# Clipping attention scores after the exponential on VectorE, in place of two ScalarE passes before it

## Chip, core and metric

The kernel runs on one core of a Trainium2 chip. The metric is device time in microseconds (us) of one execution; lower is better. The engines are TensorE (PE in the profile; PEld is its weight load), VectorE (DVE), ScalarE (ACT), GpSimd (POOL) and SyncE (SP, which issues the DMAs).

## What is computed

The reference is one cross-attention layer followed by a quantised feed-forward layer, on x of shape 8 x 1024 x 512 with a context of 8 x 64 x 512:

```python
lat = layernorm(_layernorm(x)); ctx = layernorm(context)
q = lat @ Wq; k, v = split(ctx @ Wkv)            # 16 heads of 64
attn = einsum('bhnd,bhsd->bhns', q, k) * 64 ** -0.5
attn = clip(attn, -11.0, 11.0)
attn = softmax(attn, axis=-1)
x = x + einsum('bhns,bhsd->bhnd', attn, v) @ Wo + bo
xq = fake_quant(_layernorm(x))
h = fake_quant(silu(xq @ Wg) * (xq @ Wu))
x = x + h @ Wd
```

The change is about the clip of the scores to -11 .. 11, which stands before the softmax.

## The kernel before

**Three stages.** `weights` prepares the operands (its last VectorE instructions make the bias and scale of the scores and two constants, `keep.bounds`). `attention` does the first layer in 16 steps of 512 tokens. `ffn` does the second layer.

**A step of attention.** Wq and the keys of a batch are folded into one matrix M, and the values and Wo into another, VW. Step s computes on TensorE the 8 score tiles of group s (`score`, each 128 rows, which are 16 heads x 8 context positions, by 512 tokens; 12 matmuls a tile, because each operand is split in a high and a low fp16 part). Then it computes the four output tiles of the group before (`output(s - 1, t)`, 24 matmuls each). Between them, in fixed places of TensorE's queue, stand: fold products for a coming batch (`fold_keys` in odd steps, `fold_values` in even ones: one half behind output tile 0, the other behind tile 2), `denominators(s)` inside output tile 1, and `turn_back(s)` inside output tile 2. The PSUM buffers `ring` hold four score or fold tiles; a score tile t + 4 waits until ScalarE has read tile t.

**Order on each engine.** Every engine has one queue written out by hand, and semaphores are the only link.

- ScalarE, for each tile t of the step: `cap` (Relu from PSUM, with the scale and the bias, into the fp32 tile E), `high(s - 1, t + 2)` (the fp16 high part of a probability of the group before), `floor` (Relu in place), in odd t `high_y` (high part of a normalised row of the next group), `exp` (Exp in place). `cap` and `floor` together are the clip.
- VectorE, for each t, the "score stretch": `divide(s - 1, t + 2)` (E times the inverse denominator, which is in PSUM), `low(s - 1, t + 1)` (the fp16 low part), in even t `norm_rows(s + 1, t // 2)`, in odd t `low_y(s + 1, t // 2)`. Behind the 8 tiles: `unit_range` (a range of feed-forward weights), `take(s - 1, 0)`, four fold tiles, `invert(s)` (reciprocal and expansion of the denominators, for `turn_back`), `norm_stats` and `norm_aggregates` of group s + 2, `take(s - 1, 1)`, `norm_rstd`, `take(s - 1, 2)`, four fold tiles, `divide(s, 0)`, `take(s - 1, 3)`, `divide(s, 1)`, `low(s, 0)`.
- GpSimd: `add_up(s, t)` for t = 1 .. 7 adds the exponentials of the tiles for the denominators, as they come; from t = 4 on a `bias` (adds bo to x) stands behind each; at the end `round_unit` (rounds a unit of weights, in steps 0 to 14).

`denominators(s)` waits for the seventh addition. `turn_back(s)` waits for `invert(s)`.

Of the kernel before, what the change touches and what calls it, by code (L numbers as in the profile page):

```python
# [14 lines left out]
fp32 = mybir.dt.float32  # L15
# [3 lines left out]
ALU = mybir.AluOpType  # L19
ACT = mybir.ActivationFunctionType  # L20
AX = mybir.AxisListType

P = 128
# [71 lines left out]
def weights(nc, mem, sem, keep, vecs, ctx_in, ln_c_w, ln_c_b, wq, wkv, wo, kv_d):  # L95
# [5 lines left out]
    with mem as ctx:  # L101
# [119 lines left out]
        def _(dve):  # L221
# [107 lines left out]
            for c in range(DC):  # L329
# [10 lines left out]
            do(nc.vector.tensor_tensor(sel[:].rearrange("p (n s) -> p n s", s=KS), misc[:].rearrange("p (n s) -> p n s", s=KS),  # L340
                                       keep.own_row[:].rearrange("p (a s) -> p a s", a=1).broadcast_to((P, NCTX // KS, KS)),
                                       ALU.mult))
            do(nc.vector.tensor_reduce(keep.score_bias[:], sel[:].rearrange("p (n s) -> p n s", s=KS), AX.X, ALU.add))
            do(nc.vector.tensor_scalar(keep.score_bias[:], keep.score_bias[:], -1.0, CLIP, ALU.mult, ALU.add))
            do(nc.vector.memset(keep.bounds[:, 0:1], 2 * CLIP))
            do(nc.vector.memset(keep.bounds[:, 1:2], -CLIP))

            do(nc.vector.tensor_tensor(keep.score_scale[:], sc[:, WQ, 1:2], sc[:, K, 1:2], ALU.mult))
            do(nc.vector.tensor_scalar(keep.score_scale[:], keep.score_scale[:], -1.0 / (LN_GAIN * FOLD_GAIN), None, ALU.mult))
            do(nc.vector.tensor_tensor(keep.out_scale[:], sc[:, WO, 1:2], sc[:, V, 1:2], ALU.mult))  # L350
            do(nc.vector.tensor_scalar(keep.out_scale[:], keep.out_scale[:], 1.0 / (PROB_GAIN * FOLD_GAIN), None, ALU.mult))
            nc.vector.reciprocal(keep.out_unscale[:], keep.out_scale[:])
# [126 lines left out]
def attention(nc, ctx, sem, keep, x_in, w_gate, w_up, w_down, kv_d, fold_d, x1_d, gate_up_q, down_q):  # L479
# [32 lines left out]
    fold_spilled, fold_loaded = [sem(f"fold_spilled{k}") for k in range(4)], sem("fold_loaded")  # L512
    ln_step, ln_y, y_hi, y_lo = sem("ln_step"), sem("ln_y"), sem("y_hi"), sem("y_lo")
    y_turned = [sem("y_turned0"), sem("y_turned1")]
    scores, capped, floored, exps, sums = sem("scores"), sem("capped"), sem("floored"), sem("exps"), sem("sums")
    dens, rdens, rden_turned = sem("dens"), sem("rdens"), sem("rden_turned")
    prob, prob_hi, prob_lo = sem("prob"), sem("prob_hi"), sem("prob_lo")
    x_biased, x_scaled = sem("x_biased"), sem("x_scaled")
# [119 lines left out]
    def on_gpsimd(pool):  # L638
        nc.gpsimd.memset(magic[:, 0:1], MAGIC).then_inc(magic_set, 1)
        nc.gpsimd.memset(magic[:, 1:2], -MAGIC).then_inc(magic_set, 1)  # L640

        def round_unit(u):
            n = unit_size(u)
            pool.wait_ge(f_scaled, scaled_before(u + 1))
            wait(pool, f_spilled, 16 * u)
            nc.gpsimd.tensor_scalar(quant[:, 0:n], raw[:, 0:n], MAGIC, QMAX, ALU.subtract, ALU.min).then_inc(f_rounded, 1)

        def bias(g, t):
            pool.wait_ge(ln_y, 4 * g + t + 1)
            nc.gpsimd.tensor_tensor(x[:, g % 4, t], x[:, g % 4, t], keep.bo[:], ALU.add).then_inc(x_biased, 1)  # L650

        def add_up(g, t):
            pool.wait_ge(exps, 8 * g + t + 1)
            if t == 1:
                wait(pool, dens, g)
                nc.gpsimd.tensor_tensor(esum[:], E[:, g % 2, 0], E[:, g % 2, 1], ALU.add).then_inc(sums, 1)  # L656
            else:
                pool.wait_ge(sums, 7 * g + t - 1)
                nc.gpsimd.tensor_tensor(esum[:], esum[:], E[:, g % 2, t], ALU.add).then_inc(sums, 1)  # L659

        for t in range(TT):
            bias(0, t)

        for s in range(NG):
            more = s + 1 < NG
            for t in range(1, KT):
                add_up(s, t)
                if more and t >= 4:
                    bias(s + 1, t - 4)
            if s < UNITS:  # L670
                round_unit(s)

    def on_scalar(act):
# [19 lines left out]
            elif values_folded_in(s) is not None:  # L693
                fold_value(values_folded_in(s), u)

        def cap(g, t):

            act.wait_ge(scores, 8 * g + t + 1)
            if g % 2 == 1:
                act.wait_ge(fold_spilled[t // 2], 32 * ((g - 1) // 2) + 32)  # L700
            else:
                wait(act, prob_lo, 8 * (g - 2) + t + 1)
            k = 8 * (g // 2) + t
            nc.scalar.activation(E[:, g % 2, t], ring[t % 4][:], ACT.Relu, scale=keep.score_scale[:],  # L704
                                 bias=keep.score_bias[:, k:k + 1]).then_inc(capped, 1)

        def floor(g, t):

            act.wait_ge(capped, 8 * g + t + 1)
            nc.scalar.activation(E[:, g % 2, t], E[:, g % 2, t], ACT.Relu, scale=-1.0, bias=keep.bounds[:, 0:1]).then_inc(floored, 1)  # L710

        def exp(g, t):
            act.wait_ge(floored, 8 * g + t + 1)
            nc.scalar.activation(E[:, g % 2, t], E[:, g % 2, t], ACT.Exp, bias=keep.bounds[:, 1:2]).then_inc(exps, 1)  # L714

        def high(g, t):
            act.wait_ge(prob, 8 * g + t + 1)
# [23 lines left out]
        for s in range(NG):  # L741
            more = s + 1 < NG
            for t in range(KT):
                cap(s, t)
                if s > 0 and t < 6:
                    high(s - 1, t + 2)
                floor(s, t)
                if more and t % 2 == 1:
                    high_y(s + 1, t // 2)
                exp(s, t)  # L750
            for t in range(TT):
                for u in FOLD_AFTER[t]:
                    fold(s, u)
                if t == 0 and s < UNITS:
                    scale_unit(s)
                if more and t == 1:
                    rescale(s + 1)
                if t >= 2:
                    high(s, t - 2)
# [3 lines left out]
    def on_vector(dve):  # L763
# [39 lines left out]
        def fold(s, u):  # L803
            if keys_folded_in(s) is not None:
                fold_key(keys_folded_in(s), u)
            elif values_folded_in(s) is not None:
                fold_value(values_folded_in(s), u)

        def invert(g):
            dve.wait_ge(dens, g + 1)  # L810
            nc.vector.reciprocal(rtok[:].rearrange("p t h -> p (t h)"), pd[:, 0:TT * H]).then_inc(rdens, 1)
            dve.wait_ge(rdens, 2 * g + 1)
            nc.vector.tensor_copy(rexp[:], rtok[:].rearrange("p t (h a) -> p t h a", a=1).broadcast_to((P, TT, H, KS))).then_inc(rdens, 1)

        def divide(g, t):
            if t == 0:
                dve.wait_ge(rden_turned, g + 1)
            dve.wait_ge(exps, 8 * g + t + 1)
            nc.vector.tensor_tensor(E[:, g % 2, t], E[:, g % 2, t], pd[:], ALU.mult).then_inc(prob, 1)  # L819

        def low(g, t):
# [49 lines left out]
        for s in range(NG):  # L871
            more = s + 1 < NG
            ahead = s + 2 < NG
            for t in range(KT):
                if s > 0 and t < 6:
                    divide(s - 1, t + 2)
                if s > 0 and t < 7:
                    low(s - 1, t + 1)
                if more and t % 2 == 0:
                    norm_rows(s + 1, t // 2)  # L880
                if more and t % 2 == 1:
                    low_y(s + 1, t // 2)
            if s < UNITS:
                unit_range(s)
            if s > 0:
                take(s - 1, 0)
            if more:
                for u in FOLD_AFTER[0]:
                    fold(s, u)
            invert(s)  # L890
            if ahead:
                norm_stats(s + 2)
                norm_aggregates(s + 2)
            if more:
                if s > 0:
                    take(s - 1, 1)
                for u in FOLD_AFTER[1]:
                    fold(s, u)
                if ahead:
                    norm_rstd(s + 2)  # L900
                if s > 0:
                    take(s - 1, 2)
                for u in FOLD_AFTER[2]:
                    fold(s, u)
                divide(s, 0)
                if s > 0:
                    take(s - 1, 3)
                divide(s, 1)
                low(s, 0)
# [19 lines left out]
    def on_tensor(pe):  # L929
        def ring_free(s, t):  # L930

            if s == 0:
                pe.wait_ge(m_lo, 4 + t + 1)
            elif keys_folded_in(s - 1) is not None:
                pe.wait_ge(m_lo, 8 * keys_folded_in(s - 1) + 4 + t + 1)
            elif values_folded_in(s - 1) is not None:
                pe.wait_ge(v_lo, 8 * values_folded_in(s - 1) + 4 + t + 1)
            else:
                pe.wait_ge(capped, 8 * (s - 1) + 4 + t + 1)

        def score(g, t):
            if t == 0:
# [3 lines left out]
            if t < 4:  # L946
                ring_free(g, t)
            else:
                pe.wait_ge(capped, 8 * g + t - 4 + 1)
            for c in range(DC):  # L950
                ins = split_products(nc, ring[t % 4][:], M[:, 0, c, t], M[:, 1, c, t], yT[:, g % 2, 0, c], yT[:, g % 2, 1, c],
                                     c == 0, c == DC - 1)
# [15 lines left out]
        def fold_keys(b, c):  # L968
# [4 lines left out]
            if c >= 2:  # L973
                pe.wait_ge(m_lo, 8 * b + u - 2)
            elif b > 0:
                pe.wait_ge(capped, 8 * (2 * b - 1) + 4 + u + 2)
            w = slice(c * P, (c + 1) * P)
            for q in range(IC):
                for n, (i, j) in enumerate(SPLITS):
# [9 lines left out]
        def fold_values(b, k):  # L989
# [4 lines left out]
            if k >= 2:  # L994
                pe.wait_ge(v_lo, 8 * b + u - 2)
            else:
                pe.wait_ge(capped, 8 * (2 * b) + 4 + u + 2)
            for n, (i, j) in enumerate(SPLITS):
                for h in range(2):
                    at = slice(64 * h, 64 * h + 64)  # L1000
# [388 lines left out]
def program(nc, x, ctx_in, ln_l_w, ln_l_b, ln_c_w, ln_c_b, wq, wkv, wo, bo, clip_x, clip_down, w_gate, w_up, w_down, out):  # L1389
    with ExitStack() as ctx:  # L1390
# [11 lines left out]
        keep.row_scale = sb("row_scale", [P, 2, FT], fp32)  # L1402
        keep.score_bias = sb("score_bias", [P, NCTX // KS], fp32)
        keep.score_scale = sb("score_scale", [P, 1], fp32)
        keep.bounds = sb("score_bounds", [P, 2], fp32)
        keep.out_scale = sb("out_scale", [P, 1], fp32)
        keep.out_unscale = sb("out_unscale", [P, 1], fp32)
        keep.rows = sb("x1_rows", [P, NG * TT, 4], fp32)
# [82 lines left out]
```

## Time and profile before

| | us |
|---|---|
| median of 3 runs | 1416.24 (1415.93 to 1416.41) |
| profiled execution, its own time | 1416.41 |
| its span | 1414.4 |
| PE busy | 1292.3 (91%) |
| DVE busy | 1196.6 (85%) |
| ACT busy | 788.2 (56%) |
| POOL busy | 411.0 (29%) |

How to read it: times in rows are microseconds unless marked ns. Positions are counted from the start of the span. In the timeline a row has the start, the duration, the engine, the line of the kernel, the operation, what is written from what, and, in square brackets, how long the engine sat idle before it and which instruction ended that. Consecutive instructions of one engine overlap a little (some 0.09 us on DVE), so an engine's pitch is shorter than its durations. TensorE's matmuls are shown with 0.38 us and follow each other every 0.216 us. Attention's 16 steps begin at 147.3, the last ends about 895; the first score matmul of steps 1 to 15 stands at 186.19, 233.78, 279.51, 326.05, 371.78, 418.33, 464.06, 510.60, 556.33, 603.15, 648.88, 696.56, 743.38, 791.50 and 838.32.

### The profile page before, as it was taken

How to read it: one execution, taken by the hardware profiler on the slowest of the kernel's cores; microseconds unless marked ns; L12 is line 12 of the kernel's file. 1: busy time of each engine (PE TensorE's matmuls, PEld its weight loads, DVE VectorE, ACT ScalarE, POOL GpSimd, SP SyncE). 2: the span in 40 equal slices, each digit the busy share in tenths (PEclk: the TensorE clock that was granted, in tenths of full speed). 3: DMA queues.
4: the chain of work that ended last, by engine and by line, in shares of the span. 5: the costliest groups of instructions: out<-in, count | busy, mean ns of one | idle time of the engine just before them, and what ended most of it. 6: DMA issues, size and time to landing. Idle time of an engine off the chain costs nothing.

```text
span 1414.4 us, 20500 instructions
## 1 busy us (share of the span) xinstructions
PE 1292.3 (91%) x7692; PEld 608.0 (43%) x7692; DVE 1196.6 (85%) x2053; ACT 788.2 (56%) x1179; POOL 411.0 (29%) x285
## 2 busy tenths in 40 slices
PE   4881889999999999999999999599999999889997
PEld 4430335444444444544444444244444444334433
DVE  7766589988998898888898875688999999789996
ACT  1662775577557755676567554143434333498662
POOL 3001443453245423552355232000000000035555
PEclk9995889999999999999999999899999999989999
DMA  5115352363534724546337250757666642289995
GB/s 230 60 60 180 89 178 68 112 187 107 193 89 112 216 84 138 138 125 209 92 96 217 76 153 22 201 152 258 222 212 229 244 164 86 94 319 425 425 393 209
DMA packets 178434, 242.77 MB, mean 172 GB/s; under 512 B 121368, under 2 KB 140576, under 8 KB 167328
## 3 DMA queue, kind: packets, MB, share of 16 engines
q1 hardware_dynamic: 178336, 241.47, 51.8%
q8 instruction: 60, 0.98, 0.3%
q14 instruction: 38, 0.31, 0.1%
HBM read 121.90 MB, written 90.57 MB: 150 GB/s over the span
## 4 chain that ended last, share of the span: by engine, by line
PE 37%; DVE 32%; ACT 10%; issue 5%; DMA 4%; SPq 2%; POOL 0%; POOLq 0%; ACTq 0%; DVEq 0%
PE pg L1349 10%; PE pu L1355 10%; PE pu L1383 7%; DMA yT<-y 3%; DVE y L791 3%; ACT E L710 3%; ACT E L704 3%; DVE x L830 3%; DVE st L833 3%; DVE E L800 2%; DVE st L768 2%; DVE M L795 2%; DVE E L819 2%; ACT y L677 2%; DVE w L1321 2%
## 5 line engine op out<-in xcount | busy, mean ns | idle before, releaser
L1224 ACT ACTIVATE sg<-pg,gate_scale 128x512 f32<-128x512 f32 x176 | 121.0, 687 | 187.0 <-PE pg L1349 187.0
L73 PE MATMUL ring<-yT,M 128*128 128x512 f16 x512 | 195.8, 383 | 7.0 <-DVE M L795 4.6
L74 PE MATMUL ring<-yT,M 128*128 128x512 f16 x512 | 195.8, 382 | 0.0
L75 PE MATMUL ring<-yT,M 128*128 128x512 f16 x512 | 195.7, 382 | 0.0
L1349 PE MATMUL pg<-xqT,w 128*128 128x512 bf16 x704 | 181.6, 380 | 2.8 <-DMA xqT<-xq 2.1
L73 PE MATMUL po<-VW,p 128*128 128x512 f16 x480 | 182.2, 380 | 0.0
L75 PE MATMUL po<-VW,p 128*128 128x512 f16 x480 | 181.9, 379 | 0.0
L74 PE MATMUL po<-VW,p 128*128 128x512 f16 x480 | 181.9, 379 | 0.0
L1355 PE MATMUL pu<-xqT,w 128*128 128x512 bf16 x704 | 181.5, 380 | 0.0
L1383 PE MATMUL pu<-w 128*128 128x512 bf16 x704 | 158.2, 385 | 18.8 <-DVE w L1323 10.1
L659 POOL TENSOR_TENSOR esum<-esum,E 128x512 f32<-128x512 f32 x96 | 130.3, 1357 | 77.6 <-ACT E L714 77.5
L1283 DVE TENSOR_TENSOR hb<-pu,sg 128x512 f32<-128x512 f32 x176 | 120.8, 686 | 31.0 <-PE pu L1355 29.5
L823 DVE TENSOR_TENSOR p<-E,p 128x512 f16<-128x512 f32 x120 | 140.6, 1171 | 6.6 <-ACT p L722 6.5
L1241 ACT ACTIVATE hb<-hb,magic,hscale 128x512 f32<-128x512 f32 x176 | 125.2, 802 | 32.1 <-DMA hb<-hidden 28.2
L722 ACT ACTIVATE p<-E 128x512 f16<-128x512 f32 x120 | 74.9, 625 | 97.7 <-DVE E L819 95.5
L791 DVE TENSOR_TENSOR y<-y 128x512 f16<-128x512 f32 x64 | 55.6, 869 | 74.3 <-ACT y L677 74.3
L1287 DVE TENSOR_REDUCE hmax_g<-hb 128x1 f32<-128x512 f32 x176 | 117.7, 676 | 0.0
L656 POOL TENSOR_TENSOR esum<-E 128x512 f32<-128x512 f32 x16 | 20.4, 1274 | 331.9 <-ACT E L714 331.9
L1383 PEld LDWEIGHTS pu<-w 128*128 128x128 bf16 x704 | 68.4, 99 | 108.3 <-DVE sg L1328 14.6
L1349 PEld LDWEIGHTS pg<-xqT,w 128*128 128x128 bf16 x704 | 68.8, 98 | 87.1 <-DMA xqT<-xq 3.2
L1209 POOL PARTITION_ALL_REDUCE one<-one x2 | 0.7, 352 | 362.8 <-DVE one L1308 316.9
L1355 PEld LDWEIGHTS pu<-xqT,w 128*128 128x128 bf16 x704 | 69.1, 98 | 83.7 <-issue 1.1
(200 smaller groups left out, 2260.9 us busy)
## 6 DMA issues: line engine op xcount, KB each, us to landing
hidden<-hb SPq DMA_DIRECT2D x11, 2816.0 KB, 9.8
hb<-hidden SPq DMA_DIRECT2D x11, 2816.0 KB, 19.4
xa<-x_rows_d SPq DMA_DIRECT2D x28, 1024.0 KB, 6.3
x<-in_x_dram SPq DMA_DIRECT2D x16, 1024.0 KB, 5.8
value_fold<-E SPq DMA_DIRECT2D x64, 256.0 KB, 2.5
VW<-value_fold SPq DMA_DIRECT2D x16, 1024.0 KB, 6.2
x_rows_d<-x SPq DMA_DIRECT2D x16, 1024.0 KB, 5.0
out_dram<-xa SPq DMA_DIRECT2D x12, 1024.0 KB, 13.7
```

Source lines behind the costliest of these rows:

```text
L73: nc.tensor.matmul(out, a_hi, b_hi, start=first, stop=False)
L74: nc.tensor.matmul(out, a_hi, b_lo, start=False, stop=False)
L75: return nc.tensor.matmul(out, a_lo, b_hi, start=False, stop=last)
L659: nc.gpsimd.tensor_tensor(esum[:], esum[:], E[:, g % 2, t], ALU.add).then_inc(sums, 1)
L823: nc.vector.tensor_tensor(probs(g, 1, t), E[:, g % 2, t], probs(g, 0, t), ALU.subtract).then_inc(prob_lo, 1)
L1224: nc.scalar.activation(sg[:, n % 4], pg[n % 4][:], ACT.Silu, scale=gate_scale[:, n % FT:n % FT + 1]).then_inc(silus, 1)
L1241: nc.scalar.activation(hb[:, slot, m], hb[:, slot, m], ACT.Identity, scale=hscale[:, m:m + 1], bias=magic[:, 0:1]).then_inc(h_scaled, 1)
L1283: nc.vector.tensor_tensor(hb[:, HOME[g], i], pu[n % 4][:], sg[:, n % 4], ALU.mult).then_inc(hs, 1)
L1287: nc.vector.tensor_reduce(hmax_g[:, i:i + 1], hb[:, HOME[g], i], AX.X, ALU.max, apply_absolute_value=True).then_inc(reaches, 1)
L1349: ins = nc.tensor.matmul(pg[n % 4][:], wg[:, c, at], xqT[:, g % 2, c], start=(c == 0), stop=(c == DC - 1))
L1355: ins = nc.tensor.matmul(pu[n % 4][:], wu[:, c, at], xqT[:, g % 2, c], start=(c == 0), stop=(c == DC - 1))
L1383: ins = nc.tensor.matmul(pu[t][:], hq[:, q % 2, m, t * P:(t + 1) * P], wd[:, m], start=(m == 0), stop=(m == FT - 1))
```

## The change

ScalarE's `cap` and `floor` go. `exp` reads the scores from PSUM directly (with the scale and bias that `cap` had, sign changed), and a new VectorE instruction `clip` limits the exponentials in place to exp(-11) .. exp(11): one in-place fp32 instruction of 128 x 512 with two constants for each of the 128 tiles. GpSimd's additions wait for `clip` in place of `exp`; TensorE's reuse of a PSUM buffer waits for `exp` in place of `cap`. In VectorE's queue `clip(s, t)` stands behind `norm_rows` and ahead of `low_y`. `invert(s)` is moved behind `norm_stats(s + 2)` and `norm_aggregates(s + 2)` (steps 0 to 13 have these). In `weights` three small VectorE instructions for the bias and the constants go.

```diff
-            do(nc.vector.tensor_reduce(keep.score_bias[:], ...))
-            do(nc.vector.tensor_scalar(keep.score_bias[:], keep.score_bias[:], -1.0, CLIP, ALU.mult, ALU.add))
-            do(nc.vector.memset(keep.bounds[:, 0:1], 2 * CLIP))
-            do(nc.vector.memset(keep.bounds[:, 1:2], -CLIP))
+            nc.vector.tensor_reduce(keep.score_bias[:], ...)
...
         def add_up(g, t):
-            pool.wait_ge(exps, 8 * g + t + 1)
+            pool.wait_ge(clips, 8 * g + t + 1)
...
-        def cap(g, t):
+        def exp(g, t):
             act.wait_ge(scores, 8 * g + t + 1)
...
-            nc.scalar.activation(E[:, g % 2, t], ring[t % 4][:], ACT.Relu, scale=keep.score_scale[:],
-                                 bias=keep.score_bias[:, k:k + 1]).then_inc(capped, 1)
-        def floor(g, t):
-            act.wait_ge(capped, 8 * g + t + 1)
-            nc.scalar.activation(E[:, g % 2, t], E[:, g % 2, t], ACT.Relu, scale=-1.0, bias=keep.bounds[:, 0:1]).then_inc(floored, 1)
-        def exp(g, t):
-            act.wait_ge(floored, 8 * g + t + 1)
-            nc.scalar.activation(E[:, g % 2, t], E[:, g % 2, t], ACT.Exp, bias=keep.bounds[:, 1:2]).then_inc(exps, 1)
+            nc.scalar.activation(E[:, g % 2, t], ring[t % 4][:], ACT.Exp, scale=keep.score_scale[:],
+                                 bias=keep.score_bias[:, k:k + 1]).then_inc(exps, 1)
...
             for t in range(KT):
-                cap(s, t)
+                exp(s, t)
                 if s > 0 and t < 6:
                     high(s - 1, t + 2)
-                floor(s, t)
                 if more and t % 2 == 1:
                     high_y(s + 1, t // 2)
-                exp(s, t)
...
+        def clip(g, t):
+            dve.wait_ge(exps, 8 * g + t + 1)
+            nc.vector.tensor_scalar(E[:, g % 2, t], E[:, g % 2, t], float(np.exp(CLIP)), float(np.exp(-CLIP)),
+                                    ALU.min, ALU.max).then_inc(clips, 1)
...
                     norm_rows(s + 1, t // 2)
+                clip(s, t)
                 if more and t % 2 == 1:
                     low_y(s + 1, t // 2)
...
-            invert(s)
             if ahead:
                 norm_stats(s + 2)
                 norm_aggregates(s + 2)
+            invert(s)
...
-                pe.wait_ge(capped, 8 * g + t - 4 + 1)
+                pe.wait_ge(exps, 8 * g + t - 4 + 1)
```

## Rows read from the trace of the kernel before

**Rows 1.** The page: TensorE's granted clock in fortieths of the span (9: full).

```profile
PEclk9995889999999999999999999899999999989999
```

**Rows 2.** TensorE's timeline of step 6: start, duration, instruction, idle before it.

```profile
418.33 0.38 PE L73 MATMUL ring<-yT,M 128*128 128x512 f16 x1 [0.31 <-DVE M L795]
...
453.03 0.60 PE L965 MATMUL pd<-ident,rexp 128*128 128x128 f32 x4
```

**Rows 3.** Busy time of step 6's score stretch on DVE, and of its rest.

```profile
core 0: us, PE busy (x) PEld busy (x) DVE busy (x) ACT busy (x) POOL busy (x), PEclk, DMA share, GB/s
421.90:444.16 22.26, 22.26 (x105) 9.96 (x102) 18.54 (x23) 21.40 (x35) 12.02 (x9) 1.00 0.55 159
444.16:468.11 23.95, 23.95 (x153) 11.44 (x152) 23.26 (x59) 8.54 (x13) 7.30 (x4) 1.00 0.34 102
```

**Rows 4.** DVE's timeline of step 6, and one row of step 15.

```profile
421.83 0.68 DVE L819 TENSOR_TENSOR E<-E,pd 128x512 f32<-128x512 f32 x1
422.42 0.69 DVE L823 TENSOR_TENSOR p<-E,p 128x512 f16<-128x512 f32 x1
423.03 0.54 DVE L787 TENSOR_SCALAR y<-x,mv,rs 128x512 f32<-128x512 f32 x1
...
426.89 0.69 DVE L791 TENSOR_TENSOR y<-y 128x512 f16<-128x512 f32 x1 [2.12 <-ACT y L677]
...
436.01 1.76 DVE L823 TENSOR_TENSOR p<-E,p 128x512 f16<-128x512 f32 x1
...
444.16 1.21 DVE L848 TENSOR_REDUCE row_scale<-ffn_raw 128x2 f32<-128x1024 f32 x1
445.40 1.22 DVE L850 TENSOR_SCALAR row_scale<-row_scale 128x2 f32<-128x2 f32 x1
...
446.78 0.75 DVE L830 CUSTOM_DVE_ANT_0 x<-po,x,out_scale 128x512 f32<-128x512 f32 x1
...
451.22 0.55 DVE L811 RECIPROCAL rtok<-pd 128x64 f32<-128x64 f32 x1
451.81 0.84 DVE L813 COPY rexp<-rtok 128x512 f32<-128x512 f32 x1
452.57 2.45 DVE L768 BATCH_NORM_STATS2 st<-x 128x6 f32<-128x512 f32 x4
...
455.22 0.71 DVE L830 CUSTOM_DVE_ANT_0 x<-po,x,out_scale 128x512 f32<-128x512 f32 x1
...
867.17 0.43 DVE L813 COPY rexp<-rtok 128x512 f32<-128x512 f32 x1
```

**Rows 5.** POOL's timeline of step 6, and step 11's rounding.

```profile
435.96 1.27 POOL L659 TENSOR_TENSOR esum<-esum,E 128x512 f32<-128x512 f32 x1 [1.47 <-ACT E L714]
437.19 1.72 POOL L650 TENSOR_TENSOR x<-x,bo 128x512 f32<-128x512 f32 x1
...
445.33 1.26 POOL L659 TENSOR_TENSOR esum<-esum,E 128x512 f32<-128x512 f32 x1
...
679.38 4.95 POOL L646 TENSOR_SCALAR ffn_quant<-ffn_raw 128x1408 bf16<-128x1408 f32 x1 [0.20 <-ACT ffn_raw L732]
```

**Rows 6.** DVE's timeline of ffn: the nearest instruction to `clip`.

```profile
916.59 0.43 DVE L1257 TENSOR_SCALAR xa<-xa 128x512 f32<-128x512 f32 x1
916.93 0.48 DVE L1255 TENSOR_SCALAR xa<-xa,rowq 128x512 f32<-128x512 f32 x1
```

**Rows 7.** Step 14, DVE and TensorE timelines: a late `invert`, and the next step.

```profile
824.31 2.87 DVE L813 COPY rexp<-rtok 128x512 f32<-128x512 f32 x1
...
827.24 0.66 PE L965 MATMUL pd<-ident,rexp 128*128 128x128 f32 x4 [0.87 <-DVE rexp L813]
...
841.78 0.68 DVE L819 TENSOR_TENSOR E<-E,pd 128x512 f32<-128x512 f32 x1
```

**Rows 8.** DVE's timeline at the end of `weights`.

```profile
116.33 0.20 DVE L344 TENSOR_SCALAR score_bias<-score_bias 128x64 f32<-128x64 f32 x1
...
116.82 0.16 DVE L348 TENSOR_TENSOR score_scale<-operand_scales 128x1 f32<-128x1 f32 x1
```

More of the change, by code:

```diff
@@ L342, in _ @@
                                        ALU.mult))
-            do(nc.vector.tensor_reduce(keep.score_bias[:], sel[:].rearrange("p (n s) -> p n s", s=KS), AX.X, ALU.add))
-            do(nc.vector.tensor_scalar(keep.score_bias[:], keep.score_bias[:], -1.0, CLIP, ALU.mult, ALU.add))
-            do(nc.vector.memset(keep.bounds[:, 0:1], 2 * CLIP))
-            do(nc.vector.memset(keep.bounds[:, 1:2], -CLIP))
+            nc.vector.tensor_reduce(keep.score_bias[:], sel[:].rearrange("p (n s) -> p n s", s=KS), AX.X, ALU.add)
             do(nc.vector.tensor_tensor(keep.score_scale[:], sc[:, WQ, 1:2], sc[:, K, 1:2], ALU.mult))
-            do(nc.vector.tensor_scalar(keep.score_scale[:], keep.score_scale[:], -1.0 / (LN_GAIN * FOLD_GAIN), None, ALU.mult))
+            do(nc.vector.tensor_scalar(keep.score_scale[:], keep.score_scale[:], 1.0 / (LN_GAIN * FOLD_GAIN), None, ALU.mult))
             do(nc.vector.tensor_tensor(keep.out_scale[:], sc[:, WO, 1:2], sc[:, V, 1:2], ALU.mult))
@@ L514, in attention @@
     y_turned = [sem("y_turned0"), sem("y_turned1")]
-    scores, capped, floored, exps, sums = sem("scores"), sem("capped"), sem("floored"), sem("exps"), sem("sums")
+    scores, exps, clips, sums = sem("scores"), sem("exps"), sem("clips"), sem("sums")
     dens, rdens, rden_turned = sem("dens"), sem("rdens"), sem("rden_turned")
@@ L817, in divide @@
                 dve.wait_ge(rden_turned, g + 1)
-            dve.wait_ge(exps, 8 * g + t + 1)
             nc.vector.tensor_tensor(E[:, g % 2, t], E[:, g % 2, t], pd[:], ALU.mult).then_inc(prob, 1)
@@ L938, in ring_free @@
             else:
-                pe.wait_ge(capped, 8 * (s - 1) + 4 + t + 1)
+                pe.wait_ge(exps, 8 * (s - 1) + 4 + t + 1)
         def score(g, t):
@@ L975, in fold_keys @@
             elif b > 0:
-                pe.wait_ge(capped, 8 * (2 * b - 1) + 4 + u + 2)
+                pe.wait_ge(exps, 8 * (2 * b - 1) + 4 + u + 2)
             w = slice(c * P, (c + 1) * P)
@@ L996, in fold_values @@
             else:
-                pe.wait_ge(capped, 8 * (2 * b) + 4 + u + 2)
+                pe.wait_ge(exps, 8 * (2 * b) + 4 + u + 2)
             for n, (i, j) in enumerate(SPLITS):
@@ L1404, in program @@
         keep.score_scale = sb("score_scale", [P, 1], fp32)
-        keep.bounds = sb("score_bounds", [P, 2], fp32)
         keep.out_scale = sb("out_scale", [P, 1], fp32)
```

## The prediction, made before the changed kernel was built or run

> **What bounds the kernel now.** I read the page first, then TensorE's timeline of one step, then the windows of that step and the timelines of the other engines over it. By the page's first part (in the table above) TensorE is the busiest engine and DVE the next, and TensorE's granted clock is at its full level of 2.4 GHz nearly throughout [rows 1]. In attention TensorE's matmuls stand one behind the other: in step 6 scores begin at 418.33, the next ones at 464.06, and the one wait is 0.31 us, for a fold tile of DVE [rows 2]. (Such a wait, of 0.31 to 0.57 us, stands ahead of the scores of the six even steps from 4 to 14.) So TensorE sets the step, but with hardly anything to spare: the instruction that `turn_back` needs, L813, ends at 451.81 + 0.84 = 452.65, while `turn_back` begins at 453.03 [rows 2, 4]. DVE is late first. The windows say what fills it: 18.5 of 22.3 us in the score stretch, 23.3 of 23.95 us in the rest [rows 3]. The 3.7 us that are left all lie in the score stretch, in four waits of L791 (`low_y`) for ScalarE, the longest 2.12 us [rows 4]; ScalarE itself is busy for 21.4 of these 22.3 us [rows 3].
>
> **What the DVE rows hide.** L823 takes 0.69 us at 422.42, where GpSimd is idle, and 1.76 us at 436.01, where GpSimd's addition began at 435.96 and ran 1.27 us; then GpSimd's next instruction, begun at 437.19, takes 1.72 us, since L823 ran until 437.7 [rows 4, 5]. L850, which has two elements a row, takes 1.22 us beside an addition that began at 445.33 and ran 1.26 us [rows 4, 5]. Instructions with a PSUM operand (L819, L830) and reductions (L848) keep their duration there. So these DVE instructions and GpSimd's additions exclude each other, the later one waits for the end of the earlier one, and when both wait they take turns. `clip` reads and writes SBUF, as L787 and L850 do, so I take it to be one of those that wait.
>
> The Trainium skill says the same, and it speaks against the change: "SBUF — State Buffer", section "Who interferes with whom", states that VectorE in a 2-port mode (which `tensor_scalar` can enter) or with two SBUF inputs holds a port pair that it shares with GpSimd, exclusively and for the whole instruction. By that rule `clip` is priced as below; without it the sum would be only `clip`'s own time.
>
> **The change part by part.**
>
> *ScalarE loses two passes.* In a step these are 16 instructions, some 10 us of pitch. ScalarE is not on TensorE's path; what it gives is that `high_y` comes earlier, so the four waits of `low_y`, 3.7 us a step, go, except part of the first (about 0.3 us, hidden behind a GpSimd addition). `exp` from PSUM takes the place of `cap` from PSUM, which freed the PSUM buffer; I cost that at nothing, because TensorE waited for neither.
>
> *DVE gains 8 `clip`s a step.* The nearest row is L1257, in place, fp32, two constants: 0.43 us, pitch 916.93 - 916.59 = 0.34 us [rows 6]. 8 x 0.34 = 2.7 us. Its lower bound is this, all else equal; its upper bound is that each of GpSimd's 11 additions of a step (7 sums, 4 biases) holds DVE up for its full 1.24 us of pitch.
>
> *The score stretch, walked through.* Count from the first `divide` (421.83). Pitches, durations less the overlap of 0.09, are 0.6 for L819, L823 and L791, 0.45 for L787, 0.34 for `clip` and 1.24 for a GpSimd instruction [rows 4 to 6]. Own work is 6 x 0.6 + 7 x 0.6 + 4 x 0.45 + 4 x 0.6 + 8 x 0.34 = 14.7 us, before it was 12.0. An addition starts as its `clip` ends. In even t a `divide` follows, which doesn't collide, and the next `low` waits the remaining 0.65 us. In odd t `low_y` is next in DVE's queue and takes the port before GpSimd has seen the semaphore, and then again a `low` waits 0.65. Walked so, tiles 1 to 4 cost 1.35 (`low_y` behind the first addition) + 3 x 0.7. From tile 5 on GpSimd has biases ready as well, is never idle, and four DVE instructions (`clip` 5, `low` 7, `norm_rows` 3, `low_y` 3) wait a full 1.24 each. Together 8.4 us of waits, and a stretch of 23.1 us against 22.3 before (12.0 + 6.6 of collisions + 3.7 for ScalarE) [rows 3, 4]: 0.8 us later.
>
> *Behind it.* L850 now meets the end of a bias and not the beginning of an addition: some 0.1 to 0.3 us of wait and not 1.1. DVE is at `take(s - 1, 0)` at 24.6, before at 446.78 - 421.83 = 24.95: 0.35 earlier, and at the end of the four fold tiles at 29.05. So the `clip`s by themselves cost nothing at this point: they fill the holes that ScalarE left.
>
> *`invert` moved behind the statistics.* L768 and L774 take from 452.57 to the next instruction 2.65 us [rows 4]: 29.05 + 2.65 = 31.7. Then L811 0.59 and L813 0.43, as where GpSimd is idle [rows 4] (in step 6 it took 0.84, beside GpSimd's rounding): it ends at 32.7; before it was 452.65 - 421.83 = 30.8. `turn_back` could start at 31.2 before. What is late next is `turn_back`, all of TensorE's queue behind it (outputs 2 and 3, the second fold, the next scores), and behind that DVE's `take(s - 1, 3)`, which stands ahead of `divide(s, 1)` and the next score stretch. Step 14 shows the price of this chain: L813 ended at 827.18, TensorE had waited 0.87 us for it, and the next score stretch began on DVE at 841.78, 14.6 us after [rows 7]. So a step lasts 32.7 + 14.6 = 47.3 us. `denominators` is not the limit: by the walk the seventh sum ends at 25.7, TensorE is there at 25.4, and these 0.3 us vanish in the wait for `turn_back`.
>
> *The sum.* Steps 1 to 10 took 648.88 - 186.19 = 462.7 us, 46.3 each: + 1.0 each, 10.3 us. Steps 11 to 13 took 142.6 us, 47.5 each, because rounding of a longer unit (4.95 us [rows 5]) held L813 up as in step 14; behind the statistics it is free of that, and with 0.4 us more for the longer range a step takes 47.7: + 0.5 us together. Step 14 has no statistics: 0. Step 0 has no `divide` and waits for ScalarE throughout; `turn_back(0)` comes later by the statistics but the sums come sooner, and the DVE folds behind stand after `norm_rstd` anyway: 0. In the last step DVE has no rows of a next group and GpSimd no biases, so there is room for the `clip`s: 0. `weights` ends 116.82 - 116.33 = 0.5 us earlier, and DVE is the last engine there [rows 8]: - 0.5. Together + 10.3 us. The profiled execution is 1416.41 with a span of 1414.4; 1416.4 + 10.3 = 1426.7. That execution is 0.2 above the median of the runs, which I neglect.
>
> **The rivals.** A measurement of this kernel tells 0.2%, 2.8 us, from no change.
>
> *A, the forecast*: `invert` is late by 1.0 us in a step, 1426.7. Its own range is 1419 to 1437, by an error of half a GpSimd instruction (0.6 us) a step in the walk.
>
> *B, DVE keeps up, faster.* It needs the walk to be 1.1 us too long, L813 at 31.6 or before: one collision less, for example because additions that start earlier leave GpSimd idle in tiles 5 to 7. Then TensorE alone sets the step, the 0.31 us waits of four steps go (- 1.3), and steps 11 to 13 fall to some 46.1 us since the rounding no longer meets L813: 142.6 - 138.3 = 4.3. With `weights` that is - 6.1: 1410. For it speaks that 10 us a step leave an engine that was full in the score stretch; against it that DVE's rest of the step is full at 97% [rows 3] and gets the statistics ahead of what TensorE waits for. Had the walk been right by 1.1 less but the old waits stayed, it is no change, 1414 to 1419.
>
> *C, more collisions, slower by far.* If GpSimd gets the port ahead of `low_y` in odd tiles, or the sums pack closer, two more DVE instructions a step wait 1.24: 2.5 us in each of 14 steps, + 35: 1462. The far end is all 11 additions in full, 13.6 us in place of 8.4: + 73 over 14 steps, 1499. What speaks for it is that DVE issues one more colliding instruction for each tile; against it that each GpSimd instruction can block only once.
>
> **How the numbers follow.** A 0.46, C 0.20, B faster 0.22, no change between A and B 0.12. Slower by over 0.2% is A and C: 0.66; within 0.12; faster 0.22. The time is that of A, 1426.7. The range reaches nearly to B's full gain, 1411, and above to half way between A's end and C's far part, 1452; it leaves out the last of B and the most of C.
>
> **What would show it.** In the changed trace: `clip` at 0.43 us where GpSimd is idle and up to 1.7 beside an addition; no waits of L791 for ScalarE; TensorE idle about 1.1 us before `turn_back` in steps 1 to 13, released by L813; score stretch on DVE about 23 us; first score matmuls 47.3 us apart; `weights` 0.5 us shorter. The prediction is wrong if TensorE does not wait at `turn_back` (B), or if it waits longer than 2 us there or at `denominators` for GpSimd (C).

## Result and the profile after

The changed kernel takes 1424.83 us (median of 5, 1421.88 to 1427.51), the kernel before 1415.93 us beside it: a ratio of 1.0065, 95% interval 1.0048 to 1.0083. It is slower, by 8.9 us; 10.3 were predicted.

The profiled execution took 1421.97 us, its span is 1420.2. In the changed kernel's lines L700 is `exp`, L709 `high`, L772 `norm_rows`, L776 `low_y`, L796 `clip`, L801 and L803 the two halves of `invert` (reciprocal, expansion), L808 `divide`, L812 `low`, L839 the two-element scaling in `unit_range`, L955 `turn_back`.

Busy time of each engine on its page:

```profile
PE 1283.0 (90%) x7649; PEld 606.3 (43%) x7692; DVE 1251.9 (88%) x2178; ACT 635.4 (45%) x923; POOL 416.9 (29%) x285
```

ScalarE gave 153 us of work away, VectorE took 55 on, though its 128 `clip`s have only 0.34 us of pitch each (pitch: from one start to the next), 44 us together. Where the step is held shows in TensorE's timeline, at the same place as in [rows 2], and in its waits from step 1 to the end of step 14 (in all, times, longest):

```profile
421.93 0.38 PE L73 MATMUL ring<-yT,M 128*128 128x512 f16 x1
...
458.21 0.66 PE L955 MATMUL pd<-ident,rexp 128*128 128x128 f32 x4 [1.41 <-DVE rexp L803]
...
469.30 0.38 PE L73 MATMUL ring<-yT,M 128*128 128x512 f16 x1
```

```profile
PE pd L955 <- DVE rexp L803: 17.2, 14, 1.4
```

Each of the steps 1 to 14 waits once, for `invert`, and for nothing else behind its first scores. Step 6 lasts 469.30 - 421.93 = 47.37 us; before, in steps 2 to 10, it was 45.73 (even steps) and 46.5 to 46.8 (odd ones).

VectorE in the same step, from the first `divide` to the next one, as in [rows 4]:

```profile
425.39 0.68 DVE L808 TENSOR_TENSOR E<-E,pd 128x512 f32<-128x512 f32 x1
...
427.04 0.42 DVE L796 TENSOR_SCALAR E<-E 128x512 f32<-128x512 f32 x1
...
429.27 1.62 DVE L776 TENSOR_TENSOR y<-y 128x512 f16<-128x512 f32 x1 [0.28 <-ACT y L674]
...
435.05 0.68 DVE L776 TENSOR_TENSOR y<-y 128x512 f16<-128x512 f32 x1
...
440.02 1.49 DVE L796 TENSOR_SCALAR E<-E 128x512 f32<-128x512 f32 x1
...
447.46 1.20 DVE L837 TENSOR_REDUCE row_scale<-ffn_raw 128x2 f32<-128x1024 f32 x1
448.70 1.22 DVE L839 TENSOR_SCALAR row_scale<-row_scale 128x2 f32<-128x2 f32 x1
...
454.52 2.46 DVE L753 BATCH_NORM_STATS2 st<-x 128x6 f32<-128x512 f32 x4
...
457.17 0.52 DVE L801 RECIPROCAL rtok<-pd 128x64 f32<-128x64 f32 x1
457.73 0.43 DVE L803 COPY rexp<-rtok 128x512 f32<-128x512 f32 x1
...
472.75 0.68 DVE L808 TENSOR_TENSOR E<-E,pd 128x512 f32<-128x512 f32 x1
```

The expansion ends at 458.16, 32.8 us after the first `divide` (32.7 predicted), and the next stretch begins 14.6 us later, at 472.75, 47.36 us after the first. `clip` takes 0.42 us alone and 1.49 beside an addition. Windows of the score stretch and the rest, as in [rows 3]:

```profile
425.39:447.46 22.07, 22.07 (x104) 10.05 (x103) 21.77 (x30) 12.12 (x19) 12.31 (x9) 1.00 0.63 161
447.46:472.75 25.29, 23.88 (x151) 11.10 (x150) 22.92 (x58) 8.53 (x13) 7.28 (x4) 1.00 0.36 115
```

The stretch is no longer than before: the eight `clip`s fill it (21.8 busy of 22.1) where VectorE waited for ScalarE. ScalarE fell from 21.4 to 12.1 us. The rest of the step is longer, and there lie TensorE's wait and, as its echo, a wait of VectorE for output 3 (1.47 us at 469.50).

GpSimd over the same tiles, against [rows 5] (a sum is now released by `clip`):

```profile
435.20 1.65 POOL L656 TENSOR_TENSOR esum<-esum,E 128x512 f32<-128x512 f32 x1 [0.97 <-DVE E L796]
...
439.50 1.72 POOL L647 TENSOR_TENSOR x<-x,bo 128x512 f32<-128x512 f32 x1
...
448.62 1.26 POOL L656 TENSOR_TENSOR esum<-esum,E 128x512 f32<-128x512 f32 x1
```

Whole executions of one program differ by up to 7 us. The steps repeat far better: e1 and e6, which run the same code in steps 2 to 10, took 414.23 and 414.59 us there. Each kernel was traced once. So the experiments are read by the time from the first scores of step 2 to those of step 15 ("13 steps" below) beside the ratio: 838.32 - 233.78 = 604.54 us before, 846.47 - 232.29 = 614.18 after, + 9.6. By the comparison of e1 and e6, a difference under some 0.5 us in it says nothing.

### The profile page after: what moved, and what is told of

It is laid out like the page before. It is cut to its first block, busy times and chain, and to the rows that moved or that the text cites. A ratio compares the mean times of both kernels' runs of the same rounds, so it can differ in the third digit from the quotient of the medians.

```text
span 1420.2 us, 20310 instructions
## 1 busy us (share of the span) xinstructions
PE 1283.0 (90%) x7649; PEld 606.3 (43%) x7692; DVE 1251.9 (88%) x2178; ACT 635.4 (45%) x923; POOL 416.9 (29%) x285
## 4 chain that ended last, share of the span: by engine, by line
PE 44%; DVE 39%; SPq 2%; issue 2%; ACT 2%; DMA 1%; POOL 0%; POOLq 0%; DVEq 0%; ACTq 0%
PE pg L1339 10%; PE pu L1345 10%; PE pu L1373 8%; DVE p L812 7%; DVE y L776 5%; DVE E L808 4%; PE po L73 3%; PE po L75 3%; PE po L74 3%; DVE y L772 3%; DVE E L796 3%; DVE st L753 3%; DVE x L819 2%; DVE w L1311 2%; DVE st L822 2%
## 5 line engine op out<-in xcount | busy, mean ns | idle before, releaser
L1339 PE MATMUL pg<-xqT,w 128*128 128x512 bf16 x689 | 178.6, 379 | 3.6 <-DMA xqT<-xq 1.9
L1373 PE MATMUL pu<-w 128*128 128x512 bf16 x690 | 156.5, 384 | 20.3 <-DVE w L1313 10.1
L656 POOL TENSOR_TENSOR esum<-esum,E 128x512 f32<-128x512 f32 x96 | 134.8, 1404 | 97.8 <-DVE E L796 97.8
L700 ACT ACTIVATE E<-ring,score_bias,score_scale 128x512 f32<-128x512 f32 x128 | 99.3, 776 | 85.9 <-PE ring L75 85.9
L812 DVE TENSOR_TENSOR p<-E,p 128x512 f16<-128x512 f32 x120 | 127.0, 1058 | 0.2
L709 ACT ACTIVATE p<-E 128x512 f16<-128x512 f32 x120 | 75.5, 629 | 114.0 <-DVE E L808 113.8
L647 POOL TENSOR_TENSOR x<-x,bo 128x512 f32<-128x512 f32 x64 | 101.3, 1584 | 13.8 <-DVE y L772 13.8
```

The costliest lines, as they stand in the source:

```text
L812: nc.vector.tensor_tensor(probs(g, 1, t), E[:, g % 2, t], probs(g, 0, t), ALU.subtract).then_inc(prob_lo, 1)
L1339: ins = nc.tensor.matmul(pg[n % 4][:], wg[:, c, at], xqT[:, g % 2, c], start=(c == 0), stop=(c == DC - 1))
L1373: ins = nc.tensor.matmul(pu[t][:], hq[:, q % 2, m, t * P:(t + 1) * P], wd[:, m], start=(m == 0), stop=(m == FT - 1))
```

## Experiments

Ten experiments ran, each with the kernel before beside it on the same chip; the ratio is to that one. "To before" compares the 13 steps.

| kernel | median us | ratio (95%) | 13 steps, us | to before |
|---|---|---|---|---|
| changed | 1424.83 | 1.0065 (1.0048 to 1.0083) | 614.18 | + 9.6 |
| e1, clips only | 1414.67 | 0.9994 (0.9981 to 1.0006) | 603.32 | - 1.2 |
| e2, `invert` moved only | 1428.33 | 1.0092 (1.0076 to 1.0108) | 616.88 | + 12.3 |
| e3, no biases | 1405.71 | 0.9931 (0.9914 to 0.9949) | 599.83 | - 4.7 |
| e4, clips twice | 1480.21 | 1.0456 (1.0439 to 1.0474) | 663.78 | + 59.2 |
| e5, e1 and expansion on ScalarE | 1405.20 | 0.9940 (0.9924 to 0.9957) | 595.60 | - 8.9 |
| e6, `invert` by step | 1412.32 | 0.9989 (0.9979 to 1.0000) | 602.95 | - 1.6 |
| e7, biases late | 1410.97 | 0.9977 (0.9965 to 0.9990) | 599.87 | - 4.7 |
| e8, combined | 1405.22 | 0.9939 (0.9921 to 0.9957) | 595.60 | - 8.9 |
| e9, before and expansion on ScalarE | 1405.25 | 0.9940 (0.9925 to 0.9955) | 595.60 | - 8.9 |
| e10, changed and expansion on ScalarE | 1428.35 | 1.0099 (1.0075 to 1.0122) | 615.08 | + 10.5 |

### The change taken apart: e1 and e2

e1 is the changed kernel with `invert` back in its place:

```diff
+            invert(s)
             if ahead:
                 norm_stats(s + 2)
                 norm_aggregates(s + 2)
-            invert(s)
```

> The changed kernel with invert back ahead of norm_stats and norm_aggregates; the clips stay on VectorE. Theory A (the place of invert, not the clips, is what makes a step longer): the expansion of the denominators (rexp) then ends near 31.0 us after the first divide of a step instead of 32.8, TensorE does not wait at turn_back in steps 1 to 10, and their mean length falls from 47.4 us to 46.0 to 46.1, where TensorE alone sets it; in steps 11 to 14 the long rounding holds rexp up and a step stays near 46.8. Together some 13 us less than the changed kernel, and about 1410 us, a ratio of 0.995 to 0.998 to the kernel before. Rival (the clips make VectorE the bound wherever invert stands): the steps stay above 46.8 us and the time above 1418 us.

e2 is the kernel before with the opposite edit: `invert(s)` goes behind `norm_aggregates(s + 2)`, the three ScalarE passes stay.

> The kernel before with only invert moved behind norm_stats and norm_aggregates; clip, three ScalarE passes, as before. Theory A: VectorE reaches the end of its four fold tiles at 29.4 us as before, rexp ends 2.65 + 0.59 + 0.43 later, at 33.1, and a step lasts 33.1 + 14.6 = 47.6 to 47.7 us: 1.4 us over before in steps 1 to 10, about 0.5 in steps 11 to 13. Together + 15, 1431 us, ratio 1.010, as slow as the changed kernel or slower. Rival (the clips are the cost and the move is hidden by ScalarE's and TensorE's own pace): within 3 us of the kernel before.

e1 is as fast as the kernel before; in steps 2 to 10 its even steps last 45.73 us, its odd ones 46.3 (one 46.6). e2 is 13 us slower (15 expected); its steps last 47.62 and 47.72, TensorE waits 1.6 to 1.7 us at `turn_back`, and the expansion ends 36.49 us after the first scores of the step, where it ended 34.3 to 34.9 before. `turn_back` in step 6, in e1 and in e2:

```profile
453.99 0.60 PE L955 MATMUL pd<-ident,rexp 128*128 128x128 f32 x4
```

```profile
463.26 0.66 PE L965 MATMUL pd<-ident,rexp 128*128 128x128 f32 x4 [1.67 <-DVE rexp L813]
```

So the move costs everything, and the clips on VectorE by themselves are free: the 13 steps are even 1.2 us shorter, though the whole kernel's interval holds no change. With the move in, they save 616.88 - 614.18 = 2.7 us: the expansion ends 0.26 us sooner in a step (36.49 and 36.23). The rival of e1 (clips as the bound) and that of e2 (a hidden move) both fall. e1 was expected at 1410 and came to 1414.7: its odd steps did not fall to TensorE's own 45.9 (TensorE still waits 0.2 to 0.3 us for a fold tile at their end), and steps 11 to 14 lasted 46.8 to 47.8, where 46.8 was expected.

### What fills VectorE: e3, e4 and e7

e3 leaves GpSimd's biases out:

```diff
             for t in range(1, KT):
                 add_up(s, t)
-                if more and t >= 4:
-                    bias(s + 1, t - 4)
```

> The changed kernel without GpSimd's four additions of bo a step (the bias bo is left out of x; the rescaling waits for the normalised rows in place of them). Theory A (the waits of VectorE in tiles 4 to 7 are waits for GpSimd's additions): the waits of clip 5, low 7 and norm_rows 3 shrink, the score stretch falls from 22.1 to about 20 us, rexp ends at 30.5 and a step becomes TensorE's 46.0 us with invert where the change put it: some 1410 us, 14 less than the changed kernel, ratio 0.995 to 0.998. Rival (no exclusion between the two engines; VectorE's instructions in these tiles are slow for another reason): step length 47.4 us and the time of the changed kernel, 1425.

e7 leaves nothing out and puts the four biases behind the seventh sum:

```diff
-                if more and t >= 4:
-                    bias(s + 1, t - 4)
+            if more:
+                for t in range(TT):
+                    bias(s + 1, t)
             if s < UNITS:
                 round_unit(s)
```

> The changed kernel (invert behind the statistics) with GpSimd's four bias additions of a step moved behind its seventh sum, ahead of the rounding; nothing is left out. Theory A (it is the place of the biases among the score tiles that holds VectorE, as in e3): the score stretch on VectorE falls from 22.1 to about 20 us as in e3; but the biases now run beside the weight range and the rounding ends later, at some 36 us, where it meets the copy of invert: rexp near 35.7, steps 46.5 to 47.0, so 5 to 12 us less than the changed kernel: 1413 to 1420. Rival (GpSimd's total work is what counts, wherever it stands): 47.4 us a step, 1425 us.

e3 also leaves out the four biases ahead of step 0 and lets ScalarE's rescaling wait for the normalised rows in place of the biases; e7 changes nothing else. In both, `invert` stands where the change put it, and steps 2 to 10 still fall from 47.4 to 45.73 and 45.91 us, with no wait of TensorE. Two rows of e7, VectorE at the end of the stretch of step 6 (from a first `divide` at 421.23), and the expansion:

```profile
441.50 1.21 DVE L838 TENSOR_REDUCE row_scale<-ffn_raw 128x2 f32<-128x1024 f32 x1
...
451.77 0.43 DVE L804 COPY rexp<-rtok 128x512 f32<-128x512 f32 x1
```

The stretch lasts 20.3 us, not 22.1, and the expansion ends 31.0 us after the first `divide`, not 32.8. So VectorE's waits in tiles 4 to 7 are waits for GpSimd, and where GpSimd's instructions stand decides, not how many there are. I had expected 46.5 us or more in e7, because the rounding would end later and meet the expansion. But the rounding doesn't wait for GpSimd to be free: ScalarE's scaling of the weights releases it, in e7 as in the changed kernel 30.4 us after the first scores (at 448.20), and it ended as the expansion began. Only in steps 11 to 14, where it is longer, do they meet (an expansion of 1.8 to 4.5 us, steps of 46.8 to 46.9).

e3's whole time was expected near 1410 us and came to 1405.7. Its 13 steps equal e7's, so these 4 us, like the difference between e3 and e7, lie outside of them; in the two traces e3's first scores of step 2 stand 4.0 us earlier, and its time from the last step's first scores on is 2.4 us shorter. Which part of that is the edit and which the execution was not tried.

e4 does every `clip` twice:

```diff
+            nc.vector.tensor_scalar(E[:, g % 2, t], E[:, g % 2, t], float(np.exp(CLIP)), float(np.exp(-CLIP)),
+                                    ALU.min, ALU.max).then_inc(clips1, 1)
+            dve.wait_ge(clips1, 8 * g + t + 1)
             nc.vector.tensor_scalar(E[:, g % 2, t], ...).then_inc(clips, 1)
```

> The changed kernel with every clip done twice, one behind the other (the second has no effect on the values); GpSimd is released by the second. Theory A (VectorE's stretch goes one to one into the step): 8 more instructions of 0.34 to 0.38 us pitch (with the drain for the dependency up to 0.45), 2.7 to 3.6 us more in each of steps 1 to 14, and no more collisions since GpSimd's 11 instructions are the same: + 38 to + 50 us on the changed kernel, 1463 to 1475, ratio 1.033 to 1.042. Rival 1 (each further colliding instruction meets another addition in full): up to + 1.2 us for each of tiles 4 to 7 on top, + 100 us. Rival 2 (VectorE has slack left): under + 15.

It was more than Theory A's upper end: 55 us over the changed kernel, where 38 to 50 were expected. One pair of `clip`s, and TensorE's two waits of step 6:

```profile
452.75 0.42 DVE L796 TENSOR_SCALAR E<-E 128x512 f32<-128x512 f32 x1
453.21 0.43 DVE L799 TENSOR_SCALAR E<-E 128x512 f32<-128x512 f32 x1
```

```profile
478.25 1.06 PE L952 MATMUL pd<-head_cols,esum 128*128 128x16 f32 x8 [1.73 <-POOL esum L656]
...
487.75 0.66 PE L958 MATMUL pd<-ident,rexp 128*128 128x128 f32 x4 [1.55 <-DVE rexp L806]
```

The first of a pair has a pitch of 0.46 us, so 8 cost 3.7, and the step grew by 3.8 (51.18 against 47.37; 49.6 us in the 13 steps): VectorE's own work goes one to one into the step, and next to nothing is left for further collisions. That is Theory A at its upper price. The rest lies in step 1 (52.20 us against 47.56) and in step 0, which I had not counted (40.99 us; the changed kernel's code took 36.73 in its own trace and 39.41 in e6's, where the clock was like e4's, see the last section). The wait for GpSimd's sums, which the prediction gave as a sign of rival C, appears here and not in the changed kernel.

Set side by side, the expansion's end after the first scores and the length of the step, in step 6: 36.23 and 47.37 (changed), 36.48 and 47.62 (e2), 40.05 and 51.18 (e4), and in step 14 before 35.68 and 46.82. The difference is 11.13 or 11.14 each time. In the even steps in which TensorE does not wait (e1, e3) the expansion ends at 34.3 and the step is 45.73, TensorE's own. So in even steps `invert` has slack up to 45.73 - 11.14 = 34.6 us after the first scores, and each microsecond beyond it is one of the step.

GpSimd's rounding explains two numbers that come back in kernel after kernel. In every kernel but e4 it starts 30.4 to 30.5 us after the first scores in the even steps and 30.4 to 31.0 in the odd ones, and takes 3.63 us in steps 2 to 10 and 4.95 in steps 11 to 14. A copy on VectorE that is issued while it runs ends 0.3 us after it: at 34.3 in the even steps of before, e1 and e3, just inside the slack, and at 35.7 in steps 12 and 14, 1.1 us beyond it, which by itself makes them 46.8 us long.

### Where the rest of the time lies: e5, e6, e8, e9, e10

e5 puts the expansion on ScalarE, whose queue is idle there:

```diff
-            dve.wait_ge(rdens, 2 * g + 1)
-            nc.vector.tensor_copy(rexp[:], ...).then_inc(rdens, 1)
...
+        def expand(g):
+            act.wait_ge(rdens, 2 * g + 1)
+            nc.scalar.activation(rexp[:], rtok[:]..., ACT.Copy).then_inc(rdens, 1)
...
                 if t == 0 and s < UNITS:
                     scale_unit(s)
+                if t == 0:
+                    expand(s)
```

> The kernel of e1 (clips on VectorE, invert ahead of the statistics) with the second half of invert, the expansion of the denominators from 128x64 to 128x512, on ScalarE, behind its scaling of the weights, in place of VectorE's copy. Theory A (in e1 this copy waits for GpSimd's rounding, 1.1 us in even steps and 2.0 to 3.1 us in steps 11 to 14, and that alone makes those steps 46.8 to 47.8 us long): TensorE no longer waits at turn_back anywhere, steps 11 to 14 fall to 45.7 to 46.3, the odd steps to 45.9; 4 to 6 us less than e1, some 1409 us, ratio 0.995 to 0.997. Rival (ScalarE sees the reciprocal late, or VectorE's next instruction meets the rounding in place of the copy): steps 11 to 14 stay above 46.5 and the time equals e1's.

Even better than expected (4 to 6 us less than e1; the 13 steps alone are 7.7 shorter): all steps from 1 to 14 last 45.73 or 45.91 us. In step 11 ScalarE copies in 0.63 us, beside a GpSimd rounding that held VectorE's copy for 2.30 us in e1, and TensorE's windows are full:

```profile
676.57 0.63 ACT L717 ACTIVATE rexp<-rtok 128x512 f32<-128x512 f32 x1 [2.43 <-DVE rtok L808]
```

```profile
233.00:595.00 362.00, 362.00 (x2573) 1.00 0.48 140
595.00:827.00 232.00, 232.00 (x1563) 1.00 0.46 136
```

e6 is the changed kernel with `invert` moved in steps 0 and 11 to 13 alone:

```diff
+            if not (s == 0 or 11 <= s <= 13):
+                invert(s)
             if ahead:
                 norm_stats(s + 2)
                 norm_aggregates(s + 2)
-            invert(s)
+            if s == 0 or 11 <= s <= 13:
+                invert(s)
```

> The changed kernel with invert behind the statistics in steps 0, 11, 12 and 13 alone, ahead of them in all others. Theory A (the move costs 1.3 us in steps 1 to 10, and gains in step 0, where VectorE would otherwise stand idle before the denominators, and in steps 11 to 13, where it lets the copy miss the rounding): step 0 lasts 36.7 us and not 38.8, steps 11 to 13 46.9 and not 47.4, the others as in e1: first scores to the last step's 686.0 us against 689.7 in e1 and 698.5 in the changed kernel; some 1411 us, ratio 0.996 to 0.998. Rival (the short step 0 is a matter of one execution): 689 us as e1.

This one half fell. From the first scores of step 0 to those of the last step it took 688.7 us, the rival's 689 and not 686. Steps 12 and 13 last 46.83 and 46.95 as expected, but only step 13 gains by it (47.75 in e1; step 12 was 46.83 there too). Step 11 lasts 47.75: as in e1, VectorE enters it later after the first scores than in the changed kernel (its first `divide` at 4.04 us, not 3.45), and the expansion ends at 36.52, not 35.72. Step 0 lasted 39.41 us where the changed kernel, the same program up to there, had 36.73. The rival was right: the short step 0 is not the change's, it goes with the clock of that execution (see the last section).

e8 is e5 with e7's late biases and `invert` moved in step 0 alone; e9 is the kernel before, e10 the changed kernel, each with e5's edit.

> All that should help together: clips on VectorE, the expansion on ScalarE, the biases behind the sums, invert behind the statistics in step 0 alone. Theory A: every step from 1 to 14 lasts TensorE's own 45.7 to 45.9 us, step 0 36.7; first scores to the last step's 678 us against 689.7 in e1 and 691.0 before: some 1403 us, ratio 0.990 to 0.993. Rival (the small instructions of norm_rstd, which read SBUF twice, now wait for the rounding, which ends later, and put take(s - 1, 2) and the folds off): steps above 46.5, 1413 us or more.

> The kernel before (clip in two ScalarE passes, no clips on VectorE) with the expansion of the denominators on ScalarE, as in e5. Theory A (the clips are neutral: the place they take on VectorE is the time in which it waited for ScalarE; all that e5 gained is the copy that no longer meets the rounding): every step from 1 to 14 lasts 45.7 to 46.0 us here too, first scores of step 1 to those of step 15 some 642 us as in e5 (652 before), ratio 0.993 to 0.996. Rival (e5 needs the relief of ScalarE, which is 96% busy in the score stretch of the kernel before): steps above 46.1 us, a gain of less than 5 us.

> The changed kernel (invert behind the statistics) with the expansion on ScalarE. Theory A (what TensorE waits for is VectorE's queue up to the reciprocal): the expansion ends 0.6 + 0.1 us after the reciprocal, near 36.5 us after the first scores of a step where VectorE's copy ended at 36.2: steps 1 to 10 last 47.6 us, a little more than the changed kernel's 47.4; steps 11 to 13 46.9, step 14, which has no statistics, 45.8: 1424 to 1428 us, ratio 1.006 to 1.009. Rival (the copy's collisions are what counts in the changed kernel too): steps near 46, 1408 us.

e5, e8 and e9 have the same 595.60 us and the same ratio within their intervals: in these 13 steps TensorE's own pace, from which nothing more is to be had without taking matmuls away. e8's further edits add nothing: it took the expected 678 us from the first scores to the last step's, e5 679.7, but its median is e5's and not 1403. e9 met its steps of 45.7 to 46.0 us from step 2 on; step 1 lasted 47.87, and 643.5 us from its first scores to those of step 15, not 642. TensorE ran the first 4 us of that step 1 at 1.2 GHz (granted clock 0.50), in e5 at its full clock. e9 settles what the clips are worth: with the expansion out of GpSimd's way it doesn't matter whether the clip is two ScalarE passes or one VectorE instruction. e10 settles the move: the same edit is worth nothing in the changed kernel (47.57 us a step; 1428.35 us, just above the 1424 to 1428 expected), because what is late there is the reciprocal behind the statistics. Only its step 14, which has no statistics, falls to 45.73. Any of e5, e8 and e9 beats both kernels; e9 is one moved instruction.

## Why the prediction was right, step by step

*The bound, and who is late first.* Right. TensorE set the step with nothing to spare, and the first to be late was `invert` for `turn_back`: 1.32 to 1.44 us of wait in steps 1 to 10, 1.1 predicted.

*The clips, paid for by ScalarE's relief, cost nothing by themselves.* Right, shown by e1. The waits of `low_y` for ScalarE fell from 3.7 us a step to 0.28.

*`invert` moved.* Right in place: shown by e2 (move without clips: slower) and e10. The chain of 14.6 us behind it held to 0.1 in steps 2 to 14 of the changed kernel, e2, e4 and e10 wherever TensorE waited at `turn_back` (e4's step 13 apart). The end of the expansion, 32.8 us against 32.7, is right too, but the agreement to 0.1 us is luck, as the next paragraph shows.

*The walk through the stretch.* Its mechanism held (e3, e7), in tiles 3 and 5 `low_y` does go ahead of GpSimd (at 435.05, where the addition follows at 435.20 and takes 1.65 us), but two of its sizes were off by 1 us each and cancelled. The term "8.4 us of waits" measured 7.2: a VectorE instruction that waits for an addition is longer by 0.95 to 1.1 us, not by 1.24. So the stretch is 22.1 and not 23.1 us. In return L839 met the beginning of an addition, not the end of a bias: it takes 1.22 us as before, where I had 0.1 to 0.3 of wait. With only one of the two, the expansion would have stood 1 us off, as much as the whole forecast of + 1.0 us a step.

*Steps 11 to 13.* The term that was mis-sized: + 0.5 predicted, measured 799.65 - 658.95 = 140.7 against 142.6 us, - 1.9. I had given these steps the full length of the others and 0.4 us more for the longer range. But the scaling instruction behind it has one element a row there and not two, and it did not wait: 1.1 us less on VectorE's way to `invert`. VectorE in step 11, and GpSimd's addition and rounding beside it:

```profile
684.48 1.60 DVE L837 TENSOR_REDUCE down_scale<-ffn_raw 128x1 f32<-128x1408 f32 x1
686.12 0.15 DVE L839 TENSOR_SCALAR down_scale<-down_scale 128x1 f32<-128x1 f32 x1
...
694.08 0.58 DVE L803 COPY rexp<-rtok 128x512 f32<-128x512 f32 x1
```

```profile
685.65 1.27 POOL L656 TENSOR_TENSOR esum<-esum,E 128x512 f32<-128x512 f32 x1
...
689.44 4.94 POOL L643 TENSOR_SCALAR ffn_quant<-ffn_raw 128x1408 bf16<-128x1408 f32 x1 [1.29 <-ACT ffn_raw L719]
```

And the expansion was not free of the rounding behind the statistics, as the prediction has it: the rounding ends at 694.38, the copy takes 0.55 to 0.60 us in steps 11 to 13, not 0.43, and ends at 35.7 us after the first scores, where it ended before the change in steps 11 and 12 (36.2 in step 13). So in these steps the move costs nothing: e1, without it, took 142.3 us for them, the changed kernel 140.7.

*Steps 1 to 10.* + 10.3 predicted, 658.95 - 184.73 = 474.2 against 462.7: + 11.5. All of it lies in steps 2 to 10, 1.3 us each. Step 1 had 47.59 us before and 47.56 after; before, TensorE ran its stretch from 186.97 to 190.37 at 1.2 GHz (granted clock 0.50, 10 matmuls), after, its first 5 us at the full clock. The prediction's mean of 46.3 us a step holds this one, where steps 2 to 10 had 46.1. Step 14: 46.82 both times, as predicted. *`weights`*: three instructions gone; from L343's start to that of its last reciprocal (L352 before, L349 after) the time fell from 1.97 to 117.43 - 116.07 = 1.36 us, 0.6 for 0.5. It is not seen in the total, whose start-up varies by more.

*Step 0.* 0 predicted; 36.73 against 38.90 us in the profiled executions, but this is not the change's (e6). At a like clock step 0 with the move is some 0.5 us longer than before (39.41 in e6, 38.90). With it, with 0.7 us more ahead of the first scores and 2.4 us less from the last step's scores on, that one execution's span is 5.8 us longer than that of before; the medians differ by 8.9, as the 13 steps' + 9.6 would have it. Of the 2.4 us, 2.2 lie in `ffn`, whose code is the same (1414.4 - 921.5 = 492.9 us from its first matmul to the end before, 1420.2 - 929.5 = 490.7 after). What makes that last part vary was not tried.

*The rivals.* B (VectorE keeps up) needed the expansion 1.1 us sooner by the prediction's reckoning, and 1.6 by the slack measured above (36.2 against 34.6 us). What it said of the long roundings was right in kind: free of them, steps 11 to 13 last 137.6 us in e5 against 142.6 before, 5.1 less (4.3 by B). But e5 gets this by taking the copy off VectorE. C's two further collisions didn't come.

## What to carry to other kernels

Work that is put on an engine with only holes left costs nothing as long as it fills the holes and the instruction that the bound engine waits for keeps its place. Find that instruction (here the last of `invert`, with 0.3 us of slack in an even step), and never put independent work ahead of it, even where the sum of the queue stays the same. If two engines exclude each other on SBUF, look at which instructions collide rather than at busy shares: moving one copy to a third engine was worth 9 us (0.6% of the kernel), removing two ScalarE passes 1.

## What the runs showed of the hardware

A colliding `tensor_scalar` with two elements a row waited for the addition (1.22 us, L839 in step 6), the same instruction with one element a row did not (0.15 us in step 11). The kernel before has the same pair in L850, 1.22 us in step 6 and 0.15 us in step 14, each beside an addition.

TensorE's granted clock fits the length of step 0. It stood at 1.2 GHz after the waits of the start-up, and rose at different moments in two executions of the same code, here the changed kernel and e6. Columns as in [rows 3], TensorE alone:

```profile
147.00:150.00 3.00, 2.00 (x10) 1.00 0.84 313
```

```profile
147.00:150.00 3.00, 1.96 (x5) 0.50 0.87 335
150.00:155.00 5.00, 5.00 (x16) 0.65 0.01 3
```

Five matmuls in place of ten, and step 0 is 2.7 us longer. The other kernels with `invert` behind the statistics in step 0 and all biases bear it out: e8, which also had its full clock from the first scores on (24 matmuls in the first 5 us), took 36.93 us for step 0; e2, e7 and e10, at a granted clock of 0.50 there (12 matmuls), took 39.57, 39.71 and 39.59.

In e4 a wait of 1.73 us for GpSimd's sums was followed, 1 us after its end, by more than 3 us at half clock (below), and so in all of steps 2 to 12. But the length of the wait alone doesn't decide: in step 13 a wait of 1.63 us at the same place was not followed by it, one of 2.59 us at `turn_back` was; the waits at `turn_back` of 1.55 us in the same steps of e4, of 1.4 us in the changed kernel and of 1.67 us in e2 were not followed by it (e2's granted clock from 460 to 480 us, around its wait of step 6, is 1.00). What makes the difference was not tried. Step 6 of e4:

```profile
479.20:482.40 3.20, 3.20 (x10) 0.51 0.37 106
```
